# Routed experts: a tile's weights copied by DMA within SBUF instead of by ScalarE, with four weight buffers and a third bank for results

## What is computed

```python
x = x + 0.5 * ffn(layernorm(x))
x = x + attention(layernorm(x))        # linear attention, 16 heads of 16
x = x + 0.5 * ffn(layernorm(x))        # same weights as the first

def ffn(xf):                           # xf: 8192 tokens x 256
    weights, idx = gate(xf)            # softmax over 16 experts, best 2 groups of 4, best 2 experts
    h = silu(xf @ We1[e] + be1[e]) * (xf @ We3[e] + be3[e])   # 256 -> 128, for each chosen expert e
    y = sum over the two chosen e of weight[e] * (h @ We2[e] + be2[e])
    z = (silu(xf @ ws1 + bs1) * (xf @ ws3 + bs3)) @ ws2 + bs2 # shared expert, 256 -> 256 -> 256
    return y + z
```

## Time and profile before

| | us |
|---|---|
| median of 3 runs | 1521.65 |
| lowest and highest of the runs | 1510.86, 1531.87 |
| the profiled execution, its own time | 1521.71 |
| span of the profiled execution | 1520.0 |

### The profile page before, as it was taken

How to read it: one execution, slowest core, us unless ns; L and a number is a source line. 1 busy time by engine, 2 the same in 40 slices (tenths; PEclk the granted TensorE clock), 3 DMA queues, 4 the chain that set the end, 5 groups by cost and what they waited for, 6 DMA issues and landing times.

```text
span 1520.0 us, 27580 instructions
## 1 busy us (share of the span) xinstructions
PE 1287.1 (85%) x7304; PEld 1003.6 (66%) x7304; DVE 915.0 (60%) x3386; ACT 660.5 (43%) x1474; POOL 574.2 (38%) x593
## 2 busy tenths in 40 slices
PE   5999987799998895999999989895777999998940
PEld 3565654588887774888888876653444988887820
DVE  4776544366665565777777657773443666665655
ACT  4444420366666652344333354442311766665600
POOL 2467544255554550000000004674444455554500
PEclk9998989899999998999999999997889999999975
DMA  9422214444444424111111001221115454444379
GB/s 375 139 82 85 75 68 109 127 138 142 142 142 128 125 93 125 54 57 56 56 56 42 1 0 50 83 85 66 57 57 141 135 145 141 141 141 120 111 300 363
DMA packets 93324, 173.08 MB, mean 114 GB/s; under 512 B 17496, under 2 KB 60525, under 8 KB 91891
## 3 DMA queue, kind: packets, MB, share of 16 engines
q1 hardware_dynamic: 63606, 93.25, 21.0%
q0 software_dynamic: 26112, 67.82, 12.6%
q10 hardware_dynamic: 3456, 10.25, 1.7%
HBM read 88.64 MB, written 86.79 MB: 115 GB/s over the span
## 4 chain that ended last, share of the span: by engine, by line
PE 62%; DVE 10%; another core or an unknown queue 10%; issue 6%; ACT 6%; DMA 4%; POOL 1%; DVEq 0%; ACTq 0%; POOLq 0%
PE bank L545 13%; PE bank L555 9%; PE bank L426 9%; PE bank L443 5%; PE bank L557 4%; PE bank L589 4%; PE bank L578 4%; PE bank L536 3%; PE bank L652 3%; DMA w<-routed_rows 3%; DVE xn L1168 2%; ACT rows L714 2%; PE bank L408 2%; PE bank L398 2%
## 5 line engine op out<-in xcount | busy, mean ns | idle before, releaser
L1333 POOL DMA_INDIRECT routed_rows<-xn,rdest x288 | 283.4, 984 | 302.4 <-DVE rw L1146 183.1
L545 PE MATMUL bank<-rows,att 128*128 128x128 f32 x2304 | 306.9, 276 | 0.9 <-ACT att L797 0.5
L545 PEld LDWEIGHTS bank<-rows,att 128*128 128x128 f32 x2304 | 281.5, 193 | 3.4 <-issue 2.0
L1311 POOL DMA_INDIRECT expert_rows<-rows,slots x192 | 185.6, 967 | 181.5 <-DVE slots L960 107.2
L555 PE MATMUL bank<-w,rows 128*128 x576 | 183.9, 401 | 35.7 <-DVE xn L1168 34.7
L443 PE MATMUL bank<-ws,work 128*128 128x256 f32 x512 | 154.4, 434 | 61.5 <-DVE work L1086 29.0
L1157 DVE SCALAR_TENSOR_TENSOR rows<-bank,tile_b,att 128x128 f32<-128x128 f32 x288 | 100.2, 348 | 154.2 <-ACT att L802 102.6
L797 ACT COPY att<-w 128x512 f32 x288 | 180.4, 626 | 7.4 <-issue 3.6
L1168 DVE TENSOR_SCALAR xn<-bank,rw 128x256 f32<-128x256 f32 x288 | 137.1, 476 | 51.4 <-PE bank L557 46.4
L796 ACT COPY rows<-bank 128x256 f32<-128x256 f32 x288 | 107.0, 372 | 130.7 <-PE bank L536 112.3
L443 PEld LDWEIGHTS bank<-ws,work 128*128 128x128 f32 x512 | 99.9, 215 | 95.3 <-DVE work L1086 33.1
(11 more groups left out here) (184 smaller groups left out, 2183.9 us busy)
## 6 DMA issues: line engine op xcount, KB each, us to landing
rows<-expert_rows SPq DMA_DIRECT2D x288, 130.5 KB
rows<-routed_rows SPq DMA_DIRECT2D x32, 512.0 KB, 4.8
w<-routed_rows SPq DMA_DIRECT2D x10, 1024.0 KB, 17.7
out<-xres ACTq DMA_DIRECT2D x16, 512.0 KB, 7.3
xres<-in_x SPq DMA_DIRECT2D x7, 1024.0 KB, 8.0
expert_rows<-pad SPq DMA_DIRECT2D x48, 130.5 KB, 13.4
rows<-routed_rows SPq DMA_DIRECT2D x6, 1024.0 KB, 11.7
routed_rows<-xn,rdest POOLq DMA_INDIRECT x288
```

The lines of the kernel that those rows point to most:

```text
L545: last = nc.tensor.matmul(rh_ps[t % RB][:, n * P:(n + 1) * P], m.rw13[:, t % RB, c * C + n * INTER:c * C + (n + 1) * INTER], m.rT[:, t % R ...
L1311: nc.gpsimd.indirect_dma_start(out=d.xg, out_offset=bass.IndirectOffsetOnAxis(ap=m.slots[:, b % XS, k, i:i + 1], axis=0), in_=xs[:, i, :], ...
L1333: nc.gpsimd.indirect_dma_start(out=d.yt, out_offset=bass.IndirectOffsetOnAxis(ap=m.rdest[:, n:n + 1], axis=0), in_=m.ry[:, n, :], in_offse ...
```

## The change

ACT no longer copies the weights. Instead it issues, for each tile, a DMA from `m.w13` to one of four buffers `m.rw13` (`WB = 4`; 128 partitions x 2 runs of 1 KB): four at the start of the stage, then one for tile i+4 after the silu of tile i, each with its own semaphore `rw13_in[t % WB]`, for which PE waits. The results of PE go round three banks (2, 3 and 7) instead of two. The buffers for silu move within SBUF to make room.

```diff
+WB = 4
-    m.rw13 = m.att[:, 0:RB * KC * C].rearrange("p (n w) -> p n w", n=RB)
-    m.rsilu = m.att[:, RB * KC * C:RB * (KC * C + P)].rearrange("p (n w) -> p n w", n=RB)
+    m.rsilu = part(SLOTS * ROW + RB * (C + P), RB, P)
+    m.rw13 = m.att[:, 0:WB * KC * C].rearrange("p (n w) -> p n w", n=WB)
...
-    s.rT_ready, s.rT_copied, s.rw13_copied = sem("rT_ready"), sem("rT_copied"), sem("rw13_copied")
+    s.rT_ready, s.rT_copied = sem("rT_ready"), sem("rT_copied")
+    s.rw13_in = [sem(f"rw13_in{n}") for n in range(WB)]
...
-    rT_ps, ry_ps, rh_ps = m.bank[0:2], m.bank[2:4], m.bank[4:4 + RB]
+    rT_ps, ry_ps, rh_ps = m.bank[0:2], (m.bank[2], m.bank[3], m.bank[7]), m.bank[4:4 + RB]
...  in up(r, u, between) of PE
                 if r % BATCHES == BATCHES - 1 and u == 3:
                     pe.wait_ge(s.rgated_ready, TILES * (r // BATCHES + 1))
+                    pe.wait_ge(s.ry_scaled, TILES * (r // BATCHES + 1))
...  in experts(L) of PE
-                        pe.wait_ge(s.rw13_copied, t + 1)
+                        pe.wait_ge(s.rw13_in[t % WB], 16 * (t // WB + 1))
...
-                                                        m.rw13[:, t % RB, c * C + n * INTER:c * C + (n + 1) * INTER],
+                                                        m.rw13[:, t % WB, c * C + n * INTER:c * C + (n + 1) * INTER],
...
-                        wait(pe, s.ry_scaled, y - 1)
-                        nc.tensor.matmul(ry_ps[y % 2][:, 0:C], m.rgT[:, y % RB, :],
+                        wait(pe, s.ry_scaled, y + 1 - RB)
+                        nc.tensor.matmul(ry_ps[y % RB][:, 0:C], m.rgT[:, y % RB, :],
...  the bias matmul and DVE's L1168 likewise: ry_ps[y % 2] becomes ry_ps[y % RB]
...  ACT
+            def load_weights(L, i):
+                t = L * TILES + i
+                wait(act, s.rh_ready, t + 1 - WB)
+                act.dma_start(m.rw13[:, t % WB, :].rearrange("p (c n) -> p c n", c=KC),
+                              w13[:, :, bass.ds(expert_at(i), C)]).then_inc(s.rw13_in[t % WB], 16)
+
             def experts(L):
                 act.wait_ge(s.tile_b13_copied, L + 1)
                 if L == 0:
                     act.wait_ge(s.experts_in, 16 * len(expert_loads))
+                act.wait_ge(s.scattered[2], rows_sent(L, 2 + XS * (XS_USES[2] - 1)))
+                for i in range(WB):
+                    load_weights(L, i)
                 for i in range(-2, TILES):
...
-                        nc.scalar.copy(m.rw13[:, a % RB, :].rearrange("p (c n) -> p c n", c=KC),
-                                       w13[:, :, bass.ds(expert_at(i + 2), C)]).then_inc(s.rw13_copied, 1)
...
                         nc.scalar.activation(m.rsilu[:, t % RB, :], rh_ps[t % RB][:, 0:P], ACT.Silu,
                                              bias=m.tile_b13[:, 0, i:i + 1]).then_inc(s.rsilu_ready, 1)
+                        if routed(i + WB):
+                            load_weights(L, i + WB)
```

More of the change, by code:

```diff
@@ L553, in experts @@
                         pe.wait_ge(s.rgated_ready, y + 1)
-                        wait(pe, s.ry_scaled, y - 1)
-                        nc.tensor.matmul(ry_ps[y % 2][:, 0:C], m.rgT[:, y % RB, :],
+                        wait(pe, s.ry_scaled, y + 1 - RB)
+                        nc.tensor.matmul(ry_ps[y % RB][:, 0:C], m.rgT[:, y % RB, :],
                                          m.w2[:, bass.ds(e, C)], start=True, stop=False)
-                        nc.tensor.matmul(ry_ps[y % 2][:, 0:C], m.ones3[:],
+                        nc.tensor.matmul(ry_ps[y % RB][:, 0:C], m.ones3[:],
                                          m.bias_rows[:, BE2:BE2 + E * C][:, bass.ds(e, C)],
@@ L1167, in experts @@
                         wait(dve, s.rows_out[n], 16 * (y // SLOTS))
-                        nc.vector.tensor_scalar(m.ry[:, n, :], ry_ps[y % 2][:, 0:C], m.rw[:, n:n + 1], None,
+                        nc.vector.tensor_scalar(m.ry[:, n, :], ry_ps[y % RB][:, 0:C], m.rw[:, n:n + 1], None,
                                                 ALU.mult).then_inc(s.ry_scaled, 1)
```

## The result

The changed kernel takes 1558.95 us (1557.67 to 1562.71) against 1522.46 for the kernel before: ratio 1.0247, 95% interval 1.0174 to 1.0321. The forecast was 1496 us, faster. The time lies inside the range of 1463 to 1568, but on the other side of the kernel before.

The account below looks back on a forecast made before the run. PE was taken as the bound, losing about 62 us in the routed stages to late signals. From 1521.7 us, 24 (third bank) and 14 (copy) off, 9 (transfers) and 3 (start) on: 1496 us; 8-in-10 range 1463 to 1568.

Parts of the forecast that it names:

- Third result bank: PE's wait for DVE to free a result bank shrinks: 24 us won, bounds 0 and 49.
- What is late next is the transposes' copy.: With three banks, PE's next transposes need ACT's L796, which passes by only 0.27 us.
- The copy's forecast line of 25 us: Expected sign in the profile: a new line of PE waits for ACT's L796, about 25 us in all.
- The 72 stalls of the sum: Routed stages: one PE stall in four tiles, 0.88 us lost each, 63 us over 288 tiles.
- Rival (b): The stall only moves to the transposes' copy, or delays grow; pace stays 1.87, 1525 us; chance 0.23.
- No weight copy on ACT: After a stall, silu, gating and second scaling come about 0.5 us sooner: 14 us won, bounds 0 and 14.
- the 0.20: The 0.20 us PE loses in the interval behind a stall, waiting for the second scaling, L1168.
- The transfers: Weights by DMA take 0.66 to 1.06 us of the engines a tile: 9 us cost, bounds 0 and 49.
- The issue on ACT: Issuing the weights' DMA on ACT takes 0.392 us by L896, hidden behind PE's 1.65 us: cost 0.
- The start of a stage: Four DMA issues ahead of the first L796: 3 us cost for both layers, bounds 0 and 4.6 a layer.
- The sum: All terms on the profiled execution: 1521.7 - 24 - 14 + 9 + 3 = 1496 us, pace about 1.77.
- rival (c): DMA engines become the bound in the routed stages, above 1.87 us a tile: 1556 or 1577 us; chance 0.25.

Follow-up runs that it names:

- e8: Kernel before plus the third result bank alone, weights still copied by ACT, on a late chip: 1551.1 us, ratio 1.0142.
- e5: The kernel before, without an edit, on a late chip: 1525.24 us.
- e1: Kernel before plus the third result bank alone, weights still copied by ACT, on a prompt chip: 1360.8 us, ratio 0.9983.
- e3: Kernel before plus third bank, weights neither copied nor transferred (PE reads the first expert's for every tile), prompt chip: 1355.45 us, ratio 0.9943.
- e14: The changed kernel with two result banks, weights by DMA, on a late chip: 1524.4 us, ratio 1.0113 to the kernel before.
- e2: The changed kernel with two result banks, weights by DMA, on a prompt chip: 1375.86 us, ratio 1.0126 to the kernel before.
- e6: The changed kernel, without an edit, on a late chip: 1566.77 us, ratio 1.0206 to the kernel before.
- e10: The changed kernel with half of each tile's weights transferred, PE using that half twice, late chip: 1558.26 us, ratio 1.0193 to the kernel before.
- e17: Kernel before with two 64-column memsets on POOL behind every scatter, routing stages too, prompt chip: 1516.58 us, ratio 1.1183.
- e4: Kernel before with a 256-column memset on POOL behind each scatter of the routed stages, prompt chip: 1360.77 us, ratio 1.0001.
- e9: Kernel before with a 256-column memset on POOL behind each scatter of the routed stages, late chip: 1537.97 us, ratio 1.0080.
- e11: Kernel before with two memsets (256 and 64 columns) on POOL behind each routed-stage scatter, late chip: 1473.35 us, ratio 0.9719.
- e12: Kernel before with two 256-column memsets on POOL behind each routed-stage scatter, late chip: 1473.79 us, ratio 0.9733.

## Why the prediction was wrong

**The step that failed is "Third result bank", 24 us won, bounds 0 to 49.** It measured 25 us lost (e8), outside both bounds. Two of its assumptions fell.

- "The delay stays; what changes is how much delay PE can bear." The delay isn't a constant of the chip, it is made by the kernel's own cycle. It grows with POOL's run of scatters, 4.36 us from begin to release for three and 5.86 for four (e5, e8), and the run is as long as the batch of outputs that the last hold piled up. With two banks PE was stopped early at L1168, and the fourth scatter of a cycle came by itself; with three banks it joins the run (4.34 us to 5.85 from the run's begin to the release). The earlier trace rows showed the last scatter of a run of three, and I took the 2.3 us of lateness as given.
- "What is late next is the transposes' copy." It was the gating: `L556 <- L1158`, 75.2 us in 63 times in e8. The copy's forecast line of 25 us is 5.8 us in the profile after. I had checked the slack of L796 and not that of silu and L1157, for which the output matmul waits as well.

The 72 stalls of the sum were also too many: the trace before has 51 intervals over 2.2 us.

Rival (b) said in words that the delay may "grow as PE runs further ahead and POOL gets more scatters in one run", and then priced it as no change, 1525. The mechanism was right and the price was missing: one scatter more in a run is 1.5 us.

**No weight copy on ACT, 14 us won.** No run shows this gain by itself. Where PE isn't held, the stage is 234.10 us with the copy (e1) and without it (e3). On a late chip the copy was never taken away alone. In e8, with the copy in place, the interval behind a stall (one of over 2.2 us) has a median of 1.65 us, against 1.85 in e5: the third bank alone removes the 0.20, as the prediction said in brackets, so beside it nothing was left to win. In e14, without the copy and with two banks, it is 1.65 too, but the stalls themselves are longer (2.54 us against 2.39).

**The transfers, 9 us, bounds 0 to 49.** Inside the bounds, and if anything undersized: 9 to 17 us on a late chip (e14) and 14 to 17 on a prompt one (e2), each net of what the missing copy gives. The upper bound was counted from a pace of 1.75 that stands in no row. The size of a transfer was well placed. In the changed kernel ACT's queue holds 39.3% of 200 us for 96 transfers:

```profile
q10 hardware_dynamic: 26228, 25.27, 39.3%
q1 hardware_dynamic: 13873, 12.88, 23.7%
q0 software_dynamic: 4707, 12.27, 16.9%
...
att<-w ACTq DMA_DIRECT2D x96, 256.0 KB
```

That is 0.82 us each, between 0.66 and 1.06, and the share of 0.79 to 0.81 lies in the 0.75 to 0.95 named. The Trainium skill says that all issuing engines share the same 16 DMA engines ("DMA: Bandwidth & Descriptors", "Issuing engines are not separate DMA queues"). The trace agrees: the queues of ACT, SP and POOL together take 79.9% of them. The estimate of 0.60 us a tile took the term by bytes of the Trainium skill's fit, which is stated for DMAs from GpSimd and has a fixed 2.0 us beside it. It is under the measured 0.82; the measurement decides.

**The issue on ACT**: forecast 0.392 us by L896, measured 0.623:

```profile
L792 ACTq DMA_DIRECT2D att<-w x288: 622/623/718, 291.0 to 1475.5; - x144
```

ACT stands idle for 2.5 us and more in each cycle, but that the cost is 0 is not shown. Behind a stall the issue takes the place of the copy and is as long. The interval that follows a stall has a median of 1.81 us in the changed kernel and 1.79 in e6, against 1.65 in e8, which issues nothing on ACT there, and in e10, whose issue takes 0.493. The stalls themselves are shorter in turn (2.99 and 3.08 us against 3.16 and 3.33), so what the issue costs in sum is open. Silu follows L808 after 0.27 us (403.68, 403.95), against 0.26 forecast.

**The start of a stage, 3 us**, cannot be told apart in the runs; the two routed stages hold the whole difference.

**The sum.** By the medians, third bank 25 and transfers 9 make 34 of the 36.5 us measured, each against before on its own late chip; by the ratios it is 22 and 17 of 38. The intervals are wide (11 to 32 us for the bank, 3 to 32 for the transfers), so the agreement is no proof. The time equals rival (c)'s 1556, but (c) is not what happened: it asked for DMA engines with over 1.87 us of work a tile, and they had 0.80 x 2.00 = 1.60. Halving the bytes (e10) changed nothing that can be measured. e10 loses more than e8, a pace of 2.021 against 1.979 or 12 us. Its 53 runs of four hold 0.16 us longer each, which is 8 us of it; why half the bytes lengthen a run as much as all of them is open.

## What to carry to other kernels

A buffer more does not help when the wait comes from a delay that the kernel's own bursts make: first ask what sets the delay's length, and whether running further ahead feeds it. Look for a stall that repeats with a period of several tiles, two idle readers that start together, and a run of back-to-back operations on another engine just before; then space that run out (here two small memsets, 2.8% on the chips concerned) rather than deepen the pipeline. Place them where POOL has time: behind every scatter, those of the routing stages too, two memsets cost 11.8% on a prompt chip (e17). And repeat the kernel before on each chip used: without that, e1 to e4 would have been read as a 10% gain.

## What the runs showed of the hardware that I had not expected

- The same kernel takes 1361 us on some chips and 1520 on others, each steady over many executions. In the traces the difference is the signals of PE while POOL scatters (silu 0.26 or 2.38 us late at the 90th percentile), in the routed stages (234 us each in e1, 271 and 269 in e5) and in the routing stages ahead of them (first bias matmul at 245 to 257 us, e17 aside, or at 292 to 309). What differs in the chips is open.
- On a late chip a run of scatters 1.29 us apart holds PE's signals for about 1.5 us a scatter; at a spacing of 1.47 nothing is gained (e9); at 1.56 the pace is 1.685 in place of 1.889, though silu is still up to 1.68 us late at the 90th percentile (e11); at 1.73 silu is prompt (e12). The signals of ACT and DVE get through meanwhile (e8). On prompt chips runs of eight at 1.26 us do little harm: in the routing stages of e1 PE waits 12.9 us in all for L1093, where in the kernel before on a late chip it waited 23.4 us for the same operation (L1092) and 29.0 us more for L1086.
- A 256 KB copy within SBUF took 0.82 us of all 16 DMA engines and 0.62 us of ACT to issue; half of it (e10) took 0.39 us of the engines (18.9% of 200 us for 96) and 0.49 to issue.
